# Queries projected transposed, turned there, and placed in the score operand by six DMAs in a one-core attention and MoLE kernel

## The reference

```
x = x + tanh(g_xattn) * attention(layernorm(x), ctx, ctx)
    q = (xn @ Wq.T + bq) * D**-0.5;  k = ctx @ Wk.T + bk;  v = ctx @ Wv.T + bv
    k, q = xpos(k, down), xpos(q)          # x * cos + rotate_pairs(x) * sin, by position and dimension
    softmax(q k^T) v, then @ Wo.T + bo
x = x + tanh(g_ffn) * mole2(relu(mole1(layernorm(x))))
    mole(x) = x @ W + b + (1/R) * sum_e gate_e(x) * (x @ A_e) @ B_e,  gate = softmax(x @ Rw)
```

## Time and profile before

| | |
|---|---|
| median of three runs | 584.95 us (583.15 to 585.03) |
| the profiled execution's own time | 584.23 us |
| its span | 582.4 us |
| PE busy | 522.7 us (90%) |
| DVE busy | 402.3 us (69%) |
| ACT busy | 245.5 us (42%) |
| POOL busy | 84.8 us (15%) |

### The profile page before, as it was taken

How to read it: one execution, slowest core, us unless ns; L and a number is a source line. 1 busy time by engine, 2 the same in 40 slices (tenths; PEclk the granted TensorE clock), 3 DMA queues, 4 the chain that set the end, 5 groups by cost and what they waited for, 6 DMA issues and landing times.

```text
span 582.4 us, 8570 instructions
## 1 busy us (share of the span) xinstructions
PE 522.7 (90%) x3384; PEld 399.7 (69%) x3384; DVE 402.3 (69%) x920; ACT 245.5 (42%) x405; POOL 84.8 (15%) x121
## 2 busy tenths in 40 slices
PE   2668865999999899999999899999999999999897
PEld 1545454864988488855987488856987498748687
DVE  4658465866889568958889478958888487925533
ACT  3152614364353616453364616454355526251330
POOL 2418012010020112011110112011100120010000
PEclk9965986999999999999999999999999999999898
DMA  8301010010100110010101010111002000100001
GB/s 273 98 21 37 1 37 2 0 51 1 37 1 38 37 38 2 38 49 0 38 1 57 19 37 2 38 48 32 7 1 75 0 1 2 41 35 1 1 36 37
DMA packets 6131, 18.49 MB, mean 32 GB/s; under 512 B 932, under 2 KB 1772, under 8 KB 5964
## 3 DMA queue, kind: packets, MB, share of 16 engines
q10 hardware_dynamic: 4005, 12.53, 6.2%
q1 hardware_dynamic: 2087, 5.42, 2.8%
HBM read 13.49 MB, written 4.19 MB: 30 GB/s over the span
## 4 chain that ended last, share of the span: by engine, by line
PE 68%; DVE 15%; ACT 10%; POOL 3%; issue 3%; DMA 1%; ACTq 0%; DVEq 0%; POOLq 0%
PE psF L1084 11%; PE psF L1145 10%; PE psX L1128 5%; DVE max_t L748 5%; PE psX L1199 4%; PE psX L995 4%; PE psX L1013 4%; ACT probs L536 4%; PE psO L1213 3%; ACT xn L426 3%; PE psF L1213 3%; PE psF L1216 3%; PE psO L1216 3%; PE psX L1115 3%; DVE ln_s L589 2%
## 5 line engine op out<-in xcount | busy, mean ns | idle before, releaser
L748 DVE TENSOR_REDUCE max_t<-psX 128x4 fp32r<-128x616 f32 x128 | 99.4, 795 | 5.1 <-PE psX L1128 2.1
L536 ACT ACTIVATE probs<-psX 128x1024 f32<-128x1024 f32 x64 | 64.0, 1024 | 50.9 <-PE psX L1199 50.9
L1145 PE MATMUL psF<-w_hi,h_hi 128*128 128x284 f32 (+1 forms) x240 | 72.7, 303 | 0.0
L1145 PE MATMUL psF<-w_lo,h_hi 128*128 128x284 f32 (+1 forms) x240 | 70.8, 295 | 0.0
L1145 PE MATMUL psF<-w_hi,h_lo 128*128 128x284 f32 (+1 forms) x240 | 70.7, 295 | 0.0
L1128 PE MATMUL psX<-km,qT 96*128 96x308 f32 x256 | 63.5, 335 | 5.7 <-DVE max_t L748 5.0
L1128 PEld LDWEIGHTS psX<-km,qT 96*128 96x128 f32 x256 | 47.9, 200 | 20.8 <-DVE max_t L748 12.4
L446 ACT ACTIVATE h_hi<-psF 128x512 fp32r<-128x512 f32 x59 | 34.4, 594 | 56.1 <-PE psF L1090 56.0
L326 POOL TENSOR_TENSOR x<-x,tab 128x256 f32<-128x256 f32 x32 | 22.3, 727 | 195.6 <-DMA x<-in_x_dram 195.6
L1145 PEld LDWEIGHTS psF<-w_hi,h_hi 128*128 128x128 f32 x240 | 45.7, 190 | 4.8 <-issue 4.6
L1084 PE MATMUL psF<-xT_lo,w_hi 128*128 128x512 f32 x118 | 47.0, 402 | 0.0
(11 more groups left out here) (187 smaller groups left out, 1044.2 us busy)
## 6 DMA issues: line engine op xcount, KB each, us to landing
x<-in_x_dram ACTq DMA_DIRECT2D x8, 512.0 KB, 3.4
x_ln<-in_x_dram ACTq DMA_DIRECT2D x7, 512.0 KB, 3.3
out_dram<-x ACTq DMA_DIRECT2D x7, 512.0 KB, 2.6
heads_t<-in_w_dram SPq DMA_DIRECT2D x1, 1024.0 KB, 8.2
heads_t<-in_w_dram SPq DMA_DIRECT2D x1, 994.0 KB, 4.8
tab<-in_tables_dram SPq DMA_DIRECT2D x1, 674.0 KB, 6.7
x_ln<-in_x_dram SPq DMA_DIRECT2D x1, 512.0 KB, 3.3
wkv_sb<-in_wkv_dram SPq DMA_DIRECT2D x1, 512.0 KB, 9.3
```

What stands on the lines that cost most here:

```text
L536: nc.scalar.activation(dst, psX[:, 2 * (i % 2):2 * (i % 2) + 2, :], ACT.Exp).then_inc(sc_exp.sem, 1)
L748: V.tensor_reduce(max_t[:, k, half, :].rearrange("p (h g) -> p g h", h=2)[:, 2 * j:2 * j + 2, :], psX[:, 2 * j:2 * j + 2, 0:2 * S].rearran ...
L1145: ins = mm(out_bank(d, k)[:, cs], a[:, m, tokens(k)], w[:, m, cs], start=m == 0 and i == 0, stop=m == HT - 1 and i == 2)
```

## The change

The queries are projected transposed: the weights are the stationary operand and the 512 tokens the moving one, 12 matmuls of 512 columns instead of 24 of 256. The columns of Wq are put in such an order that `psX` bank 0 gets the first and bank 1 the second number of each rotated pair. DVE makes four products with bias and table in one instruction each (`q_products`; the tables `turn`, 512 KB for each `u`, are loaded by two more DMAs), and two sums (`q_turn`). ACT rounds the two halves (`q_high`), DVE takes the rest (`q_low`), and six DMAs of 256 KB, each 128 partitions x 2 KB to 16 partitions x 16 KB, place the rows in `qT`: four from SP, two from ACT. The cosine product on POOL, the 32 transposes and their eight copies to `qT` go. Keys get the same order of dimensions, with as many instructions as before.

In the written order: in a full step `q_turn` stands ahead of the last `head_blocks`; in the second step it stands behind `head_back`. In the first step `values_bias` stands behind `key_operands`. The first two pieces of `max_scores` stand ahead of and behind `router1`, tiles 0 and 1 of the hidden layer run without scores between them, and `hidden_lora` of a tile stands half a tile later. `dynamic_dma_scratch_size=4096` is given to the program; no DMA is issued by POOL.

```diff
-        q_ev = probs[:, 0:2, :].rearrange("p a (k e) -> p (a k) e", e=E)
-        q_rc = probs[:, 2:4, :].rearrange("p a (k e) -> p (a k) e", e=E)
-        q_rs = probs[:, 4:6, :].rearrange("p a (k e) -> p (a k) e", e=E)
+        q_c, q_s = probs[:, 0:2, :], probs[:, 2:4, :]
+        qh = probs[:, 4:6, :].bitcast(F32R)
+        ql = q_c.bitcast(F32R)
...
             stage("wq", wq)
+            sp.dma_start(turn[:, 0], turns[0]).then_inc(turn_loaded.sem, 16)
...
+            def rows_of_queries(c):
+
+                for s in range(2):
+                    sp.wait_ge(q_hi.sem, q_hi.at(c, s + 1))
+                    sp.dma_start(qT[16 * s:16 * s + 16, :, :].bitcast(F32),
+                                 probs[:, 4 + s, :]).then_inc(q_rows.sem, 16)
+                for s in range(2):
+                    sp.wait_ge(q_lo.sem, q_lo.at(c, s + 1))
+                    sp.dma_start(qT[32 + 16 * s:48 + 16 * s, :, :].bitcast(F32),
+                                 probs[:, s, :]).then_inc(q_rows.sem, 16)
...
+            rows_of_queries(0)
+            sp.wait_ge(w_lo["w1"].sem, 1)
+            stage("w2a", w2[:, 0:n_w2])
+            sp.wait_ge(w_lo["wq"].sem, 1)
+            stage("w2b", w2[:, n_w2:n_w2 + W2N])
+            sp.dma_start(turn[:, 1], turns[1]).then_inc(turn_loaded.sem, 16)
             rows_of_maxima(0)
-            rows_of_maxima(1)
-            for b in range(1, B):
-                rows_of_maxima(2 * b)
-                rows_of_maxima(2 * b + 1)
+            for c in range(1, B * UB):
+                rows_of_queries(c)
+                rows_of_maxima(c)
...
-                pool.wait_ge(q_evac.sem, q_evac.at(c))
-                nc.gpsimd.tensor_tensor(
-                    q_rc.rearrange("p k (h d) -> p k h d", d=D), q_ev.rearrange("p k (h d) -> p k h d", d=D),
-                    cos_q[:, u].unsqueeze(2).to_broadcast([P, TT, H, D]), ALU.mult).then_inc(q_cos.sem, 1)
...
+            def q_high(c, first):
+
+                if not first:
+                    act.wait_ge(pv_ps.sem, pv_ps.at(c - 1))
+                for s in range(2):
+                    act.wait_ge(q_rot.sem, q_rot.at(c, s + 1))
+                    copy(qh[:, s, :], q_c[:, s, :]).then_inc(q_hi.sem, 1)
+                for s in range(2):
+                    act.wait_ge(q_hi.sem, q_hi.at(c, s + 1))
+                    act.dma_start(qT[64 + 16 * s:80 + 16 * s, :, :].bitcast(F32),
+                                  probs[:, 4 + s, :]).then_inc(q_rows.sem, 16)
...
+                if second:
+                    heads_high(d, 1)
+                q_high(c, first)
                 if first:
                     load(0, 1, 1)
+                elif not second:
+                    heads_high(d, 1)
...
-                act.wait_ge(q_rot.sem, q_rot.at(c))
-                if not first:
-                    act.wait_ge(wo_ps.sem, wo_ps.at(d))
-                for lo, done in ((0, q_hi), (64, q_hi2)):
-                    copy(split[:, :].rearrange("p (a r) -> p a r", r=KS)[:, :, lo:lo + 32],
-                         q_rc.rearrange("p k (g r) -> p (k g) r", r=32)).then_inc(done.sem, 1)
...
-                for g in QT_ACT:
-                    act.wait_ge(qT_ps.sem, qT_ps.at(c, g + 1))
-                    copy(qT[0:KS, g, :], psX[0:KS, g % 4, :]).then_inc(qT_a.sem, 1)
-                    if full and g == 1:
-                        gate2_exp(e, 1)
-                    if full and g == 3:
-                        gate2_copy(e, 1)
-                    if not first and g == 3:
-                        gate1_exp(d)
+                if full:
+                    gate2_exp(e, 1)
+                    gate2_copy(e, 1)
                 if not first:
+                    gate1_exp(d)
                     gate1_copy(d)
...
-                for f2 in range(2):
-                    heads_high(c, f2)
+                heads_high(c, 0)
+                if last:
+                    heads_high(c, 1)
...
+            def q_products(c, u):
+
+                dve.wait_ge(turn_loaded.sem, turn_loaded.at(u))
+                for s in range(2):
+                    dve.wait_ge(q_ps.sem, q_ps.at(c, s + 1))
+                    for dst, w in ((q_c, s), (q_s, 1 - s)):
+                        V.scalar_tensor_tensor(out=dst[:, w, :], in0=psX[:, s, :], scalar=bq_c[:, s:s + 1],
+                                               in1=turn[:, u, w ^ s, :], op0=ALU.add, op1=ALU.mult).then_inc(q_prod.sem, 1)
+
+            def q_turn(c):
+
+                dve.wait_ge(q_prod.sem, q_prod.at(c))
+                for s, op in enumerate((ALU.subtract, ALU.add)):
+                    V.tensor_tensor(q_c[:, s, :], q_c[:, s, :], q_s[:, s, :], op).then_inc(q_rot.sem, 1)
+
+            def q_low(c):
+
+                for s in range(2):
+                    dve.wait_ge(q_hi.sem, q_hi.at(c, s + 1))
+                    V.tensor_tensor(ql[:, s, :], q_c[:, s, :], qh[:, s, :].bitcast(F32), ALU.subtract).then_inc(q_lo.sem, 1)
...
                 if first:
-                    q_bias(c)
+                    q_products(c, u)
+                if not second:
+                    q_turn(c)
+                if first:
+                    keys_bias(b)
+                    q_low(c)
+                    rotate_keys(b)
+                elif second:
+                    head_blocks(d, 3)
+                    head_norm(d, 1)
+                    head_back(d, 1)
+                    q_turn(c)
+                    head_low(d, 1)
+                    q_low(c)
                 else:
                     head_blocks(d, 3)
                     head_norm(d, 1)
+                    q_low(c)
                     head_back(d, 1)
+                    head_low(d, 1)
                 if first:
-                    rotate_keys(b)
-                q_sine(c, u)
-                if not first:
-                    head_low(d, 1)
-                q_sum(c)
-                if u == 0:
+                    key_operands(b)
+                    values_bias(b)
+                elif u == 0:
...
+                if first:
+                    for i in range(16):
+                        reduce_max(c, i)
+                        if i == 5:
+                            ln1_stats(c + 1)
+                else:
                     gates1_shift(d)
-                q_transposed(c, 5)
-                if not first:
+                    if full:
+                        finish(e, u, 2)
                     gates1_weigh(d)
-                if full:
-                    finish(e, u, 2)
-                q_transposed(c, 7)
-                if full:
-                    finish(e, u, 3)
-                for i in range(16):
-                    reduce_max(c, i)
-                    if first and i == 5:
-                        ln1_stats(c + 1)
-                    if not first:
-                        if i % 2:
-                            h_low(d, i // 2)
+                    reduce_max(c, 0)
+                    if full:
+                        finish(e, u, 3)
+                    reduce_max(c, 1)
+                    for m in range(HT):
+                        if m < HT - 1:
+                            reduce_max(c, 2 * m + 2)
+                        h_low(d, m)
+                        if m < HT - 1:
+                            reduce_max(c, 2 * m + 3)
...
-                for k in range(TT):
-                    o_ps = psX[:, k // 2, E * (k % 2):E * (k % 2) + E]
+                for s in range(2):
                     n = 0
                     for a, w in ((xT_hi, wq_hi), (xT_lo, wq_hi), (xT_hi, wq_lo)):
                         for f in range(FT):
-                            ins = mm(o_ps, a[:, f, tokens(k)], w[:, f, :], start=n == 0, stop=n == 5)
+                            ins = mm(psX[:, s, :], w[:, f, P * s:P * s + P], a[:, f, :], start=n == 0, stop=n == 5)
                             n += 1
-                    if k % 2:
-                        ins.then_inc(q_ps.sem, 1)
+                    ins.then_inc(q_ps.sem, 1)
...
-                    pe.wait_ge(qT_a.sem, qT_a.at(c, 5 + i))
-                    pe.wait_ge(qT_v.sem, qT_v.at(c, 1 + i))
-                else:
+                if i == 0:
+                    pe.wait_ge(q_rows.sem, q_rows.at(c))
+                if i >= 2:
                     pe.wait_ge(max_red.sem, max_red.at(c, i - 1))
...
-                if not first:
+                if first:
+                    for i in range(16):
+                        max_scores(c, i)
+                        if i == 9:
+                            max_transposed(c, 0, first)
+                else:
                     transpose_x2(d)
+                    if full:
+                        out_tile(e, 3, HT - 2, HT)
                     pe.wait_ge(x1_s.sem, x1_s.at(d))
-                else:
-                    pe.wait_ge(q_evac.sem, q_evac.at(c))
-                if full:
-                    out_tile(e, 3, HT - 2, HT)
-                q_transposes(c, 0, first)
-                q_transposes(c, 1, first)
-                if not first:
```

(41 more changed lines are left out.)

118 lines of the change are left out of this document (39 added, 79 removed).

## The result

The changed kernel took 569.31 us (median of 4 runs, 568.85 to 572.06) against 584.05 us (4 runs, 582.86 to 585.03) of the kernel before in the same comparison: a ratio of 0.9758, 95% interval 0.9719 to 0.9797. A later comparison, with 6 and 12 runs, had 571.20 and 584.75 us, a ratio of 0.9792 (0.9759 to 0.9824). The forecast was 570.0. It will turn out that the sum behind it was 2.4 us too high, and that something else filled the gap.

The account below looks back on a forecast made before the run. PE was busy 90% and DVE 69%, suggesting that what leaves PE is won, priced in three kinds of step. 5.0 + 3.1 + 6.6 = 14.7 us off 584.23 gave 569.5, as a median 570.2, say 570; range 564 to 578.

Parts of the forecast that it names:

- First step: Step c = 0: `max_scores` starts at 36.0 instead of 41.44 us; 5.0 us gained (0 to 5.4).
- all hidden: Six row DMAs at 1.5 to 2 us each fit the time available, 11.7 us in the first step, without delaying PE.
- no idle time of PE ended by a DMA: Sign of a right forecast: PE has no idle time ended by a DMA at L1128, the first `max_scores`.
- The rule that I had weighed and not followed: Trainium skill: 16 neighbouring partitions reach 4 of 16 ports, 104 GB/s; 2.5 us per transfer, 15 for six, sum 573.5 us.
- Second step: Chain to `router1` 0.8 us shorter, first reductions 2.4 us earlier, less 0.1: 3.1 us gained (1 to 4).
- Full steps, ahead of `router1`: Steps c = 2 to 7: DVE's added queries' work is covered before `project_out`, so the price is nothing.
- 0.6 us of cover is left: In c = 5 `head_low` ends at 344.7, `project_out` stands behind second-layer tiles until 345.26; without cover 1.4 us a step.
- Full steps, behind `router1`: First reduction 0.75 us earlier, first scores at 316.95 instead of 318.16; 1.1 us a step (0.1 to 1.8), 6.6 in six.
- `h_low(4)` stall: DVE's 0.54 us wait at 312.63, for a `relu` behind ACT's copy of the maxima, goes as tile 4's adapter stands later.
- DVE is what counts: Behind `router1` in full steps: without DVE's two copies (2 x 0.68) and with 0.6 of waits, first reduction 0.75 us earlier.
- rows late but the change still wins: Rival, 9%: row DMAs of d us cost 6d - 11.7 in the first step; 573.5 us at 2.5, 582 at 3.0.
- break-even of 3.15 us for a DMA: Rival of a slower kernel, 5%: from 3.15 us per row DMA, losses in the first step and c = 3, 5, 7 eat all gain.

Follow-up runs that it names:

- spread rows: Changed kernel with the six row DMAs writing every second partition and the keys' rows interleaved to match: 571.72 us, from 567.61 to 573.77 (6 runs).
- put-back costs: Two kernels, each the changed one plus work in full steps: 24 PE transposes ahead of `lora2_operand`, 578.08 us; two DVE additions around `finish(2)`, 576.20 us.

## Why the prediction came out right, and where its steps were wrong

**First step: 5.0 us counted, 4.3 measured.** The keys' transposes at 27.98 and the bias' end at 35.21 were forecast at 28.7 and 36.0. Two mistakes about the DMAs worked against each other. They cost more than the 1.5 to 2 us that I took, 9 to 12 us for six: four in one queue took 2.4 us each plus latency, and the six 13.9. They also began sooner: I let the time run from 24.3, but the first was issued at 22.70, which makes 12.5 us up to the bias instead of 11.7. The wait that this leaves is 1.4 us, not "all hidden", and the sign "no idle time of PE ended by a DMA" failed. The rule that I had weighed and not followed gave 2.5 us each and was right within 0.2 us for one queue (2.3 and 2.4). Its loss of 3.3 us was too high, by 0.8 because I set it against the 11.7 us, and by 1.1 because the six took 13.9 us on two queues and not 15.

**Second step: 3.1 counted, 3.4 measured.** POOL's first `ln_v` took 0.20 us, `router1` to the first reduction fell from 6.56 to 4.38 us, `project_out` came 0.1 us sooner. The rows held `max_scores(0)` by 1.26 us, of which at most 0.3 stayed, since `x2T_low` ended at 93.57 and `router1` started at 93.87; with spread rows that 0.3 us did not appear. This too was named as a sign of an error, PE waiting for DMAs ahead of `router1`.

**Full steps, ahead of `router1`: nothing counted; with u = 1 a loss of 0.3, with u = 0 a gain of 0.2.** "0.6 us of cover is left" failed. PE's `project_out` had started at 345.09, not 345.26, so the cover was 0.4 us at most. I let the products follow the projection, but `head_low(c, 0)` stands ahead of them on DVE until 326.19, and they ended 2.2 us behind the projection instead of 1.5. From there to the end of `head_low` it was 6.28 us, against 6.3 forecast. It was named as the sign of an error, and it was one, of a small size.

**Full steps, behind `router1`: 1.1 counted; 1.15 with u = 1, 0.59 with u = 0.** The first reduction came 0.72 us sooner (forecast 0.75). The scores came 0.9 us sooner, not 1.2. My engine-by-engine story of the loop was wrong. The adapter's place did not matter, and the `h_low(4)` stall went for another reason. "DVE is what counts" is refuted by the 1.34 us that PE's transposes cost when put back: the first reduction waits for DVE's `finish(2)` and that for PE, 0.78 us that my working did not have, and from the third piece on PE runs without a gap. So the 0.72 us came near my 0.75 by another path, and that is luck. Why a u = 0 step keeps less is a reading of its scores, not tried by a kernel: there the maxima's transposes wait for the last reduction, which came only 0.29 us sooner behind `router1` (22.65 us against 22.94), and the first `values` then waits 0.64 us for ACT (before 0.45). With u = 1 the same transposes are as late, but PE has the next context's transposes ahead of `values`, and waits for nothing there. The put-back costs, 1.34 and 0.60, are prices along one chain and cannot be added.

**The sum.** 4.3 + 3.4 + 4.6 for the full steps is 12.3 us where I had 14.7. The span fell by 15.4 because the end ran 3.05 us shorter at a better granted clock, which I had not priced. By the mechanism alone the forecast would have been 572.6; that it was met within 1 us is partly luck. The rival "rows late but the change still wins" was right in its mechanism and mild in its price. The break-even of 3.15 us for a DMA was not reached; at 1.625 times the bytes the kernel is 7% slower than before, so the gain did hang on these transfers.

## What to carry to other kernels

When DMAs replace an on-chip rearrangement, count the partitions that each one writes, and if they are few, choose the row order so that one DMA reaches many. Take the time available from the first issue on one side, and on the other up to what the waiting engine would wait for next. Where two engines look level in a loop, put each side's work back separately, and read in the trace which wait grows and which shrinks: here one chain over both engines set the entry of the loop, and a story of single stalls inside it was wrong. A saving in an early step counts only if it is still there at the end of that step and the next; here over 1 us was gone by the end of the second step, and the granted clock, which came back no sooner, is the likely reason. Compare the stretches that a change does not touch as well; a clock that moves by 3 us there is easily taken for an effect.

## What the runs showed of the hardware

- A DMA of 256 KB from 128 partitions landed after 4.2 us in 16 neighbouring partitions and after 3.1 in every second of 32. Six of the first kind in one queue took 15.2 us, six into 128 partitions 5.8.
- DVE's copy of 128x1024 that reads with a stride of 16 numbers (`p a (s i)` taken as `p a i s`) took 0.70 us, as the one without.
- Two such DMAs at once to different groups of 16 partitions took 6.34 to 6.51 us in one queue, whichever the groups.
- The same last piece of the program took between 47.0 and 51.5 us in different profiles. Where it was long, the granted clock was 0.50 (1.2 GHz) for 3.4 to 10.3 us in all, in stretches of which the first began 12 to 14 us behind the tail's `project_out`. In the 10 us around it PE was busy 85% of the time in both kernels (clock 0.83 in the kernel before, 1.00 in the changed one).
- In the kernel with twice the row DMAs PE stood idle for 6.29 us in c = 3, and the granted clock was 0.50 in the 6.7 us from 246.6 us on, in which the wait ended.
